# Side-by-side pixel pairs in PSUM, group 5 added on VectorE, and the last group stored in halves

## The reference

```
x = x + conv(ln_c(x))            # ln_c: over the 24 channels, eps 1e-6
t = tokens(x)                    # (8, 4096, 24)
t = t + ffn(ln_t(t))             # ln_t: over the 24 channels, eps 1e-5
return from_tokens(t)

def conv(x):                     # a factor for each pixel, the same for all channels
    V = number of walks that visit the pixel, from a Sobel map of mean(x over channels)
    return x * (V / (V + 1e-6))

def ffn(x):                      # 24 -> 96 -> 24, operands rounded to e5m2, sums to fp16
    h = relu(qlinear(x, W1, b1))
    return qlinear(h, W2, b2)
def qlinear(x, W, b):
    return fp16(fp16(e5m2(x) @ e5m2(W).T) + e5m2(b))
```

## Time and profile before

| what | value |
|---|---|
| median of 3 runs | 71.01 us (70.59 to 73.23) |
| profiled execution | 71.21 us |
| its span, first to last instruction | 69.4 us |
| TensorE busy | 53.4 us (77%) |
| VectorE busy | 54.9 us (79%) |
| ScalarE busy | 44.2 us (64%) |
| GpSimd busy | 24.1 us (35%) |
| mean granted TensorE clock | 0.948 of full |

### The profile page before, as it was taken

How to read it: one execution, slowest core, us unless ns; L and a number is a source line. 1 busy time by engine, 2 the same in 40 slices (tenths; PEclk the granted TensorE clock), 3 DMA queues, 4 the chain that set the end, 5 groups by cost and what they waited for, 6 DMA issues and landing times.

```text
span 69.4 us, 1372 instructions
## 1 busy us (share of the span) xinstructions
PE 53.4 (77%) x486; PEld 37.7 (54%) x486; DVE 54.9 (79%) x120; ACT 44.2 (64%) x60; POOL 24.1 (35%) x25
## 2 busy tenths in 40 slices
PE   2993999999999999948859969899898989700000
PEld 1323999999999999817126427355532644600000
DVE  2059934989799999999999999999999999981000
ACT  0802241161789999238999999999999998510000
POOL 1000000009885004034199989846640326000000
PEclk9999999999999999999999999999999999995555
DMA  0899995000094900653903999989999979963940
GB/s 0 291 403 404 413 402 232 9 0 0 0 184 71 198 0 0 130 101 57 170 9 73 216 218 282 209 189 200 302 218 202 296 214 331 240 241 125 395 177 11
DMA packets 4619, 12.51 MB, mean 180 GB/s; under 512 B 512, under 2 KB 640, under 8 KB 4608
## 3 DMA queue, kind: packets, MB, share of 16 engines
q0 software_dynamic: 2016, 5.51, 39.6%
q1 hardware_dynamic: 2160, 5.90, 22.2%
q10 hardware_dynamic: 432, 0.97, 3.6%
HBM read 3.72 MB, written 3.15 MB: 99 GB/s over the span
## 4 chain that ended last, share of the span: by engine, by line
PE 28%; DVE 23%; issue 15%; ACT 15%; DMA 7%; SPq 1%; DVEq 0%; ACTq 0%
ACT hidden_rounded L426 10%; PE ps_ffn L546 8%; DMA pixels<-in_x 7%; PE ps_ffn L534 6%; PE ps_ffn L564 4%; PE ps_hidden L564 4%; DVE hidden_q L852 3%; PE ps_ffn L619 3%; DVE hidden_act L843 3%; DVE result L812 3%; ACT packed_t L417 2%; DVE packed L831 2%; ACT ffn_rounded L436 2%; DVE inv_std L788 2%; DVE inv_std L817 2%
## 5 line engine op out<-in xcount | busy, mean ns | idle before, releaser
L426 ACT ACTIVATE hidden_rounded<-ps_hidden 128x1024 f16<-128x1024 f32 x24 | 23.9, 1049 | 0.5 <-PE ps_hidden L597 0.5
L343 POOL TENSOR_TENSOR result<-centred,gain 128x768 f32<-128x768 f32 x5 | 9.4, 1887 | 17.3 <-DVE scaled_var L805 14.7
L597 PE MATMUL ps_hidden<-packed_t,w1q 96*128 96x512 fp8e5 x48 | 13.9, 380 | 1.7 <-ACT packed_t L417 1.2
L331 POOL DMA_DIRECT2D result<-pixels x8 | 9.1, 1131 | 9.1 <-DVE result L812 7.9
L843 DVE TENSOR_SCALAR hidden_act<-hidden_rounded,b1q 128x1024 f16<-128x1024 f16 x24 | 11.6, 487 | 0.1
L395 ACT ACTIVATE squares<-centred 128x768 f32<-128x768 f32 (+1 forms) x9 | 6.7, 764 | 5.2 <-DVE centred L774 5.2
L619 PEld LDWEIGHTS ps_ffn<-w2q,hidden_q 128*128 128x128 fp8e5 x168 | 7.5, 98 | 3.7 <-DVE hidden_q L852 2.0
L619 PE MATMUL ps_ffn<-w2q,hidden_q 128*128 128x96 fp8e5 x168 | 8.3, 206 | 1.3 <-DVE square_sums L781 1.2
L337 POOL DMA_DIRECT2D result<-ffn_out x6 | 6.5, 1082 | 7.6 <-DVE ffn_out L860 7.6
L564 PEld LDWEIGHTS ps_ffn<-squares,fixed 128*128 128x128 f32 x72 | 8.7, 191 | 0.6
L564 PE MATMUL ps_ffn<-squares,fixed 128*128 128x128 f32 x72 | 8.9, 276 | 0.0
(11 more groups left out here) (54 smaller groups left out, 53.8 us busy)
## 6 DMA issues: line engine op xcount, KB each, us to landing
pixels<-in_x SPq DMA_DIRECT2D x8, 384.0 KB, 6.5
result<-pixels POOLq DMA_DIRECT2D x8, 384.0 KB, 4.6
out<-result SPq DMA_DIRECT2D x7, 384.0 KB, 4.3
result<-ffn_out POOLq DMA_DIRECT2D x6, 384.0 KB, 5.4
fixed<-in_fixed ACTq DMA_DIRECT2D x1, 497.5 KB, 5.5
out<-result ACTq DMA_DIRECT2D x1, 384.0 KB, 3.2
fixed<-in_fixed ACTq DMA_DIRECT2D x1, 64.0 KB, 3.3
```

The source lines that it names most:

```text
L331: pool.dma_start(result[:, n], pixels[:, n], accum_op=ALU.add).then_inc(s.residual[n], 16)
L343: nc.gpsimd.tensor_tensor(result[:, n], centred[:, n], group_values(gain, n), ALU.mult).then_inc(s.conv_pool, 1)
L426: nc.scalar.activation(hidden_rounded[:, i % HIDDEN_BUFS], ps_hidden[:, i % 2], ACT.Copy).then_inc(s.hidden_rounded, 1)
L597: last = nc.tensor.matmul(ps_hidden[:, i % 2, b * BANK:(b + 1) * BANK], w1q[:, t * P:(t + 1) * P], packed_t[:, n % 2].bitcast(E5M2)[:, b:: ...
```

## The change

Four things are changed. The second layer writes column m of pair j and pixel b to place (j, m, b) of its bank, so that a matmul's output has a step of two fp32 and the copy of ScalarE is one run of 384 per bank on both sides. The ffn result of group 5 is added on VectorE and no longer by DMA. Group 7's add and store are split into two halves by channels (SyncE stores the first, ScalarE the second), where its two bias halves, by pixels, come first, both. The written-out orders of all engines are changed: the flag is computed last, GpSimd's pixel add of group 7 is issued last, and a number of steps ahead of the steady part change places.

```diff
-ADD_BY_DMA = range(0, 6)
-ADD_ON_VECTOR = range(6, NG)
+ADD_BY_DMA = range(0, 5)
+ADD_ON_VECTOR = range(5, NG)
...
+        def ffn_pairs(n, half):
+            return ffn_banks(n)[:, half, 0:JP * CQ].rearrange("p (j m b) -> p j m b", j=JP // 2, b=2)
...
-        def wait_result(eng, s, n):
+        def wait_result(eng, s, n, part):
             if n in ADD_BY_DMA:
                 eng.wait_ge(s.residual[n], 32)
             else:
-                eng.wait_ge(s.result_vector, ADD_ON_VECTOR.index(n) + len(pixel_halves(n)))
+                eng.wait_ge(s.result_vector, ADD_ON_VECTOR.index(n) + part + 1)
+
+        def channel_parts(n):
+            return [(0, CH), (CH, C)] if n == NG - 1 else [(0, C)]
...
-            def store(s, n):
-                wait_result(sp, s, n)
-                sp.dma_start(out[n], result[:, n]).then_inc(s.stored, 16)
+            def store(s, n, part=0):
+                lo, hi = channel_parts(n)[part]
+                wait_result(sp, s, n, part)
+                sp.dma_start(out[n][:, lo:hi], result[:, n, lo:hi]).then_inc(s.stored, 16)
...
-                nc.scalar.activation(ffn_rounded[:, n % 2].rearrange("p (h j) m b -> p h b (j m)", h=2)[:, lo:hi],
-                                     ffn_banks(n)[:, lo:hi, 0:JP * CQ].rearrange("p h (b m) -> p h b m", b=2),
+                nc.scalar.activation(ffn_rounded[:, n % 2].rearrange("p (h j) m b -> p h (j m b)", h=2)[:, lo:hi],
+                                     ffn_banks(n)[:, lo:hi, 0:JP * CQ],
                                      ACT.Copy).then_inc(s.ffn_rounded, 1)
+            def store_last(s):
+                wait_result(act, s, NG - 1, 1)
+                act.dma_start(out[NG - 1][:, CH:C], result[:, NG - 1, CH:C]).then_inc(s.stored, 16)
...
-                        last = nc.tensor.matmul(ffn_banks(n)[:, half, at * CQ:(at + 1) * CQ],
+                        last = nc.tensor.matmul(ffn_pairs(n, half)[:, j, :, b],
...
-                lo, hi = [at * GPIX // 2 for at in pixel_halves(n)[part]]
+                lo, hi = channel_parts(n)[part]
                 dve.wait_ge(s.residual[n], 16)
-                dve.wait_ge(s.ffn_out, n + 1 + part)
-                total = result[:, n, :, lo:hi]
-                nc.vector.tensor_tensor(total, total, ffn_out[:, n, :, lo:hi], ALU.add).then_inc(s.result_vector, 1)
+                dve.wait_ge(s.ffn_out, n + len(pixel_halves(n)))
+                total = result[:, n, lo:hi, :]
+                nc.vector.tensor_tensor(total, total, ffn_out[:, n, lo:hi, :], ALU.add).then_inc(s.result_vector, 1)
```

More of the change, by code:

```diff
@@ L305, in _, with first_groups @@
         def _(sp):
-            def store(s, n):
-                wait_result(sp, s, n)
-                sp.dma_start(out[n], result[:, n]).then_inc(s.stored, 16)
+            def store(s, n, part=0):
+                lo, hi = channel_parts(n)[part]
+                wait_result(sp, s, n, part)
+                sp.dma_start(out[n][:, lo:hi], result[:, n, lo:hi]).then_inc(s.stored, 16)
+            def first_groups(s):
+                store(s, 0)
+                store(s, 1)
+                store(s, 2)
+                store(s, 3)
+                store(s, 4)
+                store(s, 5)
+                store(s, 6)
+                store(s, 7, 0)
             for n in range(NG):
                 sp.dma_start(pixels[:, n], x[n]).then_inc(pixels_in[n], 16)
-            for n in range(NG - 1):
-                store(flat_pass, n)
+            first_groups(flat_pass)
             uneven_map = is_uneven(sp)
-            sp.wait_ge(flat_pass.stored, 16 * NG)
+            sp.wait_ge(flat_pass.stored, 16 * (NG + 1))
             with sp.If(uneven_map):
                 for n in range(NG):
-                    store(uneven_pass, n)
-                sp.wait_ge(uneven_pass.stored, 16 * NG)
+                    for part in range(len(channel_parts(n))):
+                        store(uneven_pass, n, part)
+                sp.wait_ge(uneven_pass.stored, 16 * (NG + 1))
         @block.gpsimd
@@ L361, in first_groups @@
                 add_pixels(s, 3)
-                pool.wait_ge(s.ffn_out, 1)
+                add_ffn_by_dma(s, 0)
+                pool.wait_ge(s.hidden_q, 4)
                 conv(s, 4)
-                add_ffn_by_dma(s, 0)
                 add_pixels(s, 4)
@@ L518, in _ @@
             first_groups(flat_pass)
-            wait_result(act, flat_pass, NG - 1)
-            act.dma_start(out[NG - 1], result[:, NG - 1]).then_inc(flat_pass.stored, 16)
             uneven_map = is_uneven(act)
@@ L1039, in groups @@
                     if n in ADD_ON_VECTOR:
-                        for part in range(len(pixel_halves(n))):
+                        for part in range(len(channel_parts(n))):
                             add_ffn(s, n, part)
@@ L1071, in first_groups @@
                 inverse_std(2)
+                bias_relu(s, 0, 0)
+                conv_gain(s, 2)
                 bias_relu(s, 0, 1)
[L1073 removed]
+                conv(s, 2)
+                second_inverse(s, 2)
                 quantise_hidden(s, 0, 0, 2)
[L1075 removed]
                 bias_relu(s, 0, 2)
[L1077 removed]
+                second_norm(s, 2)
                 quantise_hidden(s, 0, 2, 3)
[L1079 removed]
+                quantise(s, 2)
+                take_var(3)
+                conv(s, 3)
+                inverse_std(3)
                 bias_relu(s, 1, 0)
[L1081 to L1082 removed]
+                conv_gain(s, 3)
                 bias_relu(s, 1, 1)
[L1084 removed]
+                second_bias(s, 0)
                 quantise_hidden(s, 1, 0, 2)
[L1086 to L1088 removed]
+                bias_relu(s, 1, 2)
+                quantise_hidden(s, 1, 2, 3)
                 quantise(s, 3)
                 second_inverse(s, 3)
[L1091 to L1092 removed]
                 bias_relu(s, 2, 0)
@@ L1112, in first_groups @@
                 bias_relu(s, 4, 2)
-                conv(s, 7)
                 quantise_hidden(s, 4, 0, 2)
@@ L1120, in first_groups @@
                 quantise_hidden(s, 5, 0, 2)
+                bias_relu(s, 6, 0)
+                quantise_hidden(s, 5, 2, 3)
                 unevenness()
-                quantise_hidden(s, 5, 2, 3)
-                bias_relu(s, 6, 0)
                 second_bias(s, 4)
                 bias_relu(s, 6, 1)
+                conv(s, 7)
                 bias_relu(s, 6, 2)
@@ L1134, in first_groups @@
                 quantise_hidden(s, 7, 2, 3)
-                flag()
+                add_ffn(s, 5)
                 second_bias(s, 6)
@@ L1138, in first_groups @@
                 second_bias(s, 7, 0)
+                second_bias(s, 7, 1)
                 add_ffn(s, 7, 0)
-                second_bias(s, 7, 1)
                 add_ffn(s, 7, 1)
+                flag()
             nc.vector.memset(table_warm[:], 1.0)
```

87 lines of the change are left out of this document (37 added, 50 removed).

## The result

The changed kernel took 73.61 us in the median (73.17 to 74.27, 4 runs), the kernel before 72.12 measured with it (70.59 to 73.52). Some executions of any kernel fall into a slower state, so ratios here compare the undisturbed runs alone (70.59 and 71.01 of the kernel before): 1.038, 95% interval 1.025 to 1.051. The forecast was 68.3 us, and 66.9 to 70.6 for its range. The profiled execution took 74.03 us, its span 72.2.

A forecast was written before the change was run, and what follows sets the result against it. The end was taken as bound by a DMA chain behind group 5's accumulation, with VectorE nearly continuous before it. Last landing at 66.1 instead of 69.0 saves 2.9: 71.21 - 2.9 = 68.3 us, range 66.9 to 70.6.

The forecast's parts named there:

- ScalarE's copy: Copy from PSUM, contiguous on both sides: 0.20 us saved on each of seven full copies, bounds 0 and 0.23.
- The landing of the last half store: ScalarE's store of group 7's second half at the end: lands 3.2 us after issue, bounds 2.7 and 5.1.
- The step that failed first: Second layer on TensorE: writing every second fp32 costs zero, matmuls staying at 43 ns.
- The rival: Step in PSUM doubles second-layer matmul time: 69.9 to 71.6 us, say 70.7, no measurable change; chance 0.10.
- a result on the slower side: Second-layer matmuls slowed above 2.2 times by the PSUM step, making the kernel over 2% slower; chance 0.06.
- The second failed step: End of program: flag ready at 63.6, its read by all engines done while stores land, over 2 us later.
- give-back: Shorter ScalarE copies cut VectorE's waits between 37 and 59 us: 0.4 us returned, bounds 0 and 1.0.
- VectorE's tail: From the last hidden_q to the last result: 4.26 us instead of 3.86, with group 5's add included.
- Reordering: New engine orders, mainly ahead of 37 us: costed at zero, bounds -0.3 and +1.0 us.
- the third rival: New order opens a hole on VectorE ahead of 37 us: 69.7 us if all of it is exposed; chance 0.08.
- the second rival: Late pixel add of group 7, or a ScalarE copy no shorter, costs half a microsecond: 68.8 us; chance 0.14.
- the forecast's terms: Whole kernel: last result at 62.8, 0.1 to issue, 3.2 to land gives 66.1; then 0.4 to the end.

The follow-up runs named there:

- e5: Kernel before with the tail parts alone (group 5 added on VectorE, group 7's bias halves first, add and store in channel halves): 68.69 us, ratio 0.978.
- e1: Changed kernel with contiguous second-layer columns and ScalarE's old copy pattern, flag still last: 71.01 us, ratio 1.009.
- e9: Changed kernel with the flag early and the second layer writing runs of two fp32 with gaps of two: 68.87 us, ratio 0.977.
- e2: Changed kernel with the flag computed early, as before, and the step of two in PSUM kept: 72.14 us, ratio 1.026.
- e4: Kernel before with the pair layout in PSUM and its copy alone, old order and tail: 74.93 us, ratio 1.065.
- e8: Changed kernel with the flag early and the second layer writing with a step of four fp32: 72.03 us, one run.
- e3: Changed kernel with contiguous columns, the old copy and the flag early; new order and tail parts kept: 69.30 us, ratio 0.985.
- e12: As e1, but with the flag's read and the second pass taken out of every engine's program: 69.02 us, ratio 0.971.
- e7: As e3, but ScalarE's copy interleaves on its read side and writes one contiguous run: 68.72 us, ratio 0.976.
- e10: As e1, but with the flag's read and the second pass taken out of TensorE's program alone: 70.12 us, ratio 0.995.
- e11: As e5, with the copy of e7 that interleaves while reading; old order, flag early: 69.11 us, ratio 0.982.

## Why the prediction was wrong, point by point

The reading of the kernel before was right: it ended with a store queued behind one accumulating DMA. e5 takes that chain away alone and gains 2.2% (1.0 to 3.3). It has 68.69 us, and the forecast without the 0.4 us that ScalarE's copy was to give back is 68.7. The landing of the last half store was sized at 3.2 us; it was 1.9 in the changed kernel and 2.9 in e5. The 2.45 us beside it was worked out from the Trainium skill ("DMA: Bandwidth & Descriptors", Anatomy of one DMA), whose figures there are for DMAs that GpSimd issues; this store is issued by ScalarE, and in the runs it landed after 1.9 to 3.1 us.

**The step that failed first** is the one on TensorE: "I take zero, since 43 ns is the time of streaming 96 columns". 43 ns holds for outputs that are contiguous or come in pairs (e1, e9); with the step of two or four it is 81 ns (the changed kernel, e2, e4, e8). The rival was named, with its doubled time, and was given 0.10; a result on the slower side was given 0.06, and only for matmuls of 2.2 times. It came with 1.9 times, because the flag's price stands on top. The rival was also sized low: 70.7 is 2.4 us above the forecast, with 3.3 at most, and the step alone costs 3.3 (e9 to e2). The rival set the extra 1.03 us of a group (0.92 measured) against TensorE's mean idle time, and that time was not where it was needed: TensorE's last matmul of a group comes 0.9 us later, ScalarE waits there, up to 1.12 us in a group, and VectorE behind it. From 37 to 56 us TensorE of the changed kernel is still idle for 19 - 17.48 = 1.5 us, while the two others wait for it. Idle time on average covers a longer step only if it lies directly in front of the one who waits.

**The second failed step** is the flag: "finishes while the stores are in flight", 63.6 against a landing more than 2 us later. The forecast named the readers and took the flag's being there as their being done; from the flag to the end of the program it is 5.0 us, longer than the 1.9 to 3.1 us of the half stores. No row of the kernel before had a price for it, since the flag was ready there at 59.38, ten microseconds ahead of the end. It costs 1.7 us (e1 to e3) or 2.0 us (e1 to e12).

**ScalarE's copy**: the size was near (0.20 taken, with 0.23 as the bound; 0.26 measured by e4, 0.23 by e7). The give-back of 0.4 lies within what was measured (0.7 in the new order with contiguous columns, none that can be told in the old), and in the changed kernel none of it shows. That the broken read or the stepped write was the cause was left open; e7 shows the write.

**VectorE's tail**: 4.26 us forecast; 4.15 in e1, where the flag is last too, 4.55 in e5 with the flag's 0.38 ahead. In the changed kernel it is 4.68, since VectorE waited 0.42 us for the second half of group 7.

**Reordering** was taken at zero, within bounds of -0.3 to 1.0. With contiguous columns the new order feeds VectorE 0.65 us later than the old one (e5 to e3), and the idle time of VectorE ahead of 37 us is 0.6 us more: the third rival was in part true. The intervals of the two times, 0.967 to 0.990 and 0.977 to 0.993, overlap. With the step it feeds it 0.80 us earlier (e4 to e2). The new order suits the slower second layer, and is no gain without it. The late pixel add of group 7, in the second rival, did no harm: it was issued at 57.56, landed 4.6 us later, and VectorE wanted it at 65.74.

**The sum.** In the profiled execution the span was 72.2 us where the forecast's terms give 66.5 (66.1 and 0.4 to the end). The 5.7 us between them are: first matmul 0.37 later; last hidden_q 2.78 later by what happens in the kernel, and the 0.40 of give-back on top; tail of VectorE 0.42 longer; from the last result to the end 1.73 longer (5.43 instead of 3.7). Of the 5.3 us that the median missed by, 4.3 are the layout and the flag. The other 1.0 is e3's distance from 68.3. Its last result came 1.13 us after the forecast's 62.8: fed 0.64 later, the tail 0.29 longer with the flag in it again, no give-back (0.40), and the first matmul 0.20 earlier.

## What to carry to other kernels

A matmul's output pattern is part of its price: single fp32 values with a step double it, pairs do not, so the interleaving belongs to the reader of PSUM, whose broken-up read cost nothing that shows here, while its write with a step did. Before an edge at the end of a program is removed, list everything that still follows the last result, the branches on a flag as well as the stores, because what they cost is invisible as long as something longer covers them. When a doubtful cost has no row in the trace, its exposure is read from who waits for that very step, not from its engine's idle share.

## What the runs showed of the hardware

- 24 matmuls of 128x96 (fp8e5, fp32 in PSUM) at a granted clock of 1.00 (2.4 GHz): 1.03 us contiguous, 1.03 us in runs of two with gaps of two, 1.95 us with a step of two, 1.95 us with a step of four.
- A ScalarE copy of 128x768 from PSUM to fp16: with one run per bank on both sides 811 ns in the mean beside the slow second layer (changed kernel) and 856 beside the fast one (e9); with alternating reads 192 fp32 apart 851 (e7); with a stepped fp16 write 1068 (before) and 1084 (e3).
- From a flag in SBUF to the end of the program, with every engine reading it and branching over the second pass: 5.0 us; 4.0 us with TensorE's read and second pass left out of its program (e10). Instruction packets move on the DMA queues in that time.
- ScalarE's last store of 192 KB landed 1.9 us behind its issue in the changed kernel, and 2.6 to 3.1 us in the ten other kernels that split it (e1, e2, e3, e5, e7, e8, e9, e10, e11 and e12). The cause is open.
